# Nine layers in one kernel: the values products of attention in bursts of two key tiles, and four probability buffers in place of two

## The reference

```python
x = _layernorm(x + _L0_attn_ref(x, ...))     # recurrent mix
x = _layernorm(x + _L0_ffn_ref(x, ...))      # selected linear layer
x = _layernorm(x + _L1_attn_ref(x, ...))     # attention, no mask      (L = 0 in the kernel)
x = _layernorm(x + _L1_ffn_ref(x, ...))      # mixture of experts
x = _layernorm(x + _L2_attn_ref(x, ...))     # attention, causal       (L = 1)
x = _layernorm(x + _L2_ffn_ref(x, ...))      # attention, causal (L = 2), then a mixture
x = _layernorm(x + _L3_attn_ref(x, ...))     # attention, causal, with slopes (L = 3)
x = _layernorm(x + _L3_ffn_ref(x, ...))
# each attention, per block and head:
energy = jnp.einsum('bqhd,bkhd->bhqk', q, k) * scale
attn = jax.nn.softmax(energy, axis=-1)
out = jnp.einsum('bhqk,bkhd->bqhd', attn, v)
```

## Time and profile before

| | |
|---|---|
| median of three runs | 1397.71 us |
| span of the profiled execution | 1397.3 us |
| TensorE matmul busy | 1237.3 us (89%) |
| VectorE busy | 929.2 us (66%) |
| ScalarE busy | 712.3 us (51%) |
| mean granted TensorE clock | 0.957 of full speed |

### The profile page before, as it was taken

The page is one execution under the profiler, slowest core; times in us unless marked ns, Lnnn a source line. Parts: engine busy times, 40 slices in busy tenths (PEclk is TensorE's granted clock), DMA queues, the critical chain, the costliest instruction groups (busy, mean ns, idle before and its releaser), DMA issues.

```text
span 1397.3 us, 26983 instructions
## 1 busy us (share of the span) xinstructions
PE 1237.3 (89%) x8574; PEld 669.9 (48%) x8574; DVE 929.2 (66%) x2118; ACT 712.3 (51%) x1300; POOL 268.8 (19%) x557
## 2 busy tenths in 40 slices
PE   3445999999889998999999999999999979999876
PEld 1222223323356655455555555556665645555445
DVE  5867768686555556667767776755554576668676
ACT  2221777767544433656666666663222226666643
POOL 2342111111000012222322232110000211221112
PEclk7667999999999999999999999999999989999988
DMA  8212231310000003323323222100000202221000
GB/s 211 113 68 69 94 113 36 119 48 6 1 1 1 0 1 119 104 87 104 102 88 124 76 66 78 41 4 3 1 0 1 74 12 67 76 80 39 3 1 31
DMA packets 65199, 79.07 MB, mean 57 GB/s; under 512 B 5611, under 2 KB 58068, under 8 KB 64602
## 3 DMA queue, kind: packets, MB, share of 16 engines
q1 hardware_dynamic: 65098, 77.80, 17.6%
HBM read 45.17 MB, written 31.72 MB: 55 GB/s over the span
## 4 chain that ended last, share of the span: by engine, by line
PE 66%; issue 12%; DVE 8%; ACT 4%; DMA 3%; DVEq 3%; POOL 2%; POOLq 1%; SPq 1%; ACTq 0%
PE bank L1591 11%; PE bank L1605 11%; PE bank L1575 9%; PE bank L1757 6%; PE bank L1758 6%; PE bank L1775 5%; PE bank L1560 3%; PE bank L1578 3%; PE bank L1593 2%; DVE M L1175 2%; DMA KS<-scr_k 2%; PE bank L1625 2%; PE bank L1496 1%; PE bank L1490 1%; PE bank L1556 1%
## 5 line engine op out<-in xcount | busy, mean ns | idle before, releaser
L1175 DVE TENSOR_REDUCE M<-bank 128x1 f32<-128x512 f32 (+3 forms) x784 | 485.1, 653 | 191.7 <-PE bank L1578 133.4
L905 ACT ACTIVATE PT<-bank 128x512 f32<-128x512 f32 (+1 forms) x784 | 429.9, 569 | 258.5 <-PE bank L1593 186.7
L1575 PE MATMUL bank<-KS,QS 125*128 125x512 bf16 (+3 forms) x1024 | 308.0, 328 | 27.5 <-DVE M L1175 18.1
L1591 PE MATMUL bank<-QS,KS 128*128 128x512 bf16 (+3 forms) x1024 | 303.3, 323 | 13.6 <-ACT PT L905 7.5
L1605 PE MATMUL bank<-PT,VA 128*32 128x512 f32 (+3 forms) x2048 | 211.7, 485 | 1.6 <-ACT PT L905 1.0
L1591 PEld LDWEIGHTS bank<-QS,KS 128*128 128x128 bf16 x1024 | 99.3, 98 | 227.1 <-ACT PT L905 155.0
L1578 PE MATMUL bank<-maskb,identb 128*128 128x128 bf16 x768 | 151.4, 223 | 0.0
L1575 PEld LDWEIGHTS bank<-KS,QS 125*128 125x128 bf16 x1024 | 101.0, 99 | 101.5 <-DVE M L1175 46.0
L1593 PE MATMUL bank<-identb,maskb 128*128 128x128 bf16 x768 | 147.8, 219 | 0.0
L1775 PEld LDWEIGHTS bank<-MW,PT 128*128 128x128 f32 x864 | 111.8, 193 | 40.8 <-issue 38.2
L1757 PE MATMUL bank<-XT,MW 128*128 128x512 f32 (+1 forms) x232 | 120.6, 601 | 10.2 <-DVE PT L1349 5.9
(11 more groups left out here) (227 smaller groups left out, 1447.5 us busy)
## 6 DMA issues: line engine op xcount, KB each, us to landing
scr_q<-PQ SPq DMA_DIRECT2D x48, 384.0 KB, 3.2
QS<-scr_q SPq DMA_DIRECT2D x64, 288.0 KB
scr_k<-PK SPq DMA_DIRECT2D x24, 384.0 KB, 3.5
KS<-scr_k SPq DMA_DIRECT2D x32, 288.0 KB
QS<-MSB SPq DMA_DIRECT2D x192, 4.0 KB
MW<-in_m_w SPq DMA_DIRECT2D x3, 1024.0 KB, 9.5
MW<-in_m_w SPq DMA_DIRECT2D x3, 832.0 KB
scr_k<-PK SPq DMA_DIRECT2D x24, 96.0 KB, 1.9
```

The lines of the kernel that those rows point to most:

```text
L905: a.activation(PT[kt % 2][:, js[0]:js[-1] + 1, q0:T], tiles(bank[st_bank(L, g, i)][:, 0:w * len(js)], len(js)), ACT.Exp, scale=c["scale"]) ...
L1175: v.tensor_reduce(M[g % 2][:, t * GH + js[0]:t * GH + js[-1] + 1], tiles(bank[S_ORDER[L][i]][:, 0:kl * len(js)], len(js)), AX_X, ALU.max, ...
L1575: r = mm(s, QS[0:ROWS_SHIFT, g * GH + j, t * P:(t + 1) * P], KS[0:ROWS_SHIFT, kv_slot(L, g, j), 0:kl], start=True, stop=not causal)
L1591: r = mm(s, KS[:, kv_slot(L, g, j), kt * P:(kt + 1) * P], QS[:, g * GH + j, T - w:T], start=True, stop=not causal)
```

## The change

The probabilities get four buffers, one for each key tile, and the wait of ScalarE moves with them: key tile kt may be written once the product of tile kt of the unit before is done. The values products of tiles 0 and 1 are issued together at step 9, those of tiles 2 and 3 together at step 1 of the next unit. The two more buffers take 16 KB of each SBUF partition; the reserve for descriptors that GpSimd would write is cut to 1024 bytes to make room. All of the kernel's transfers are issued by SyncE.

```diff
+VALUES_HERE, VALUES_REST, VALUES_REST_AT = (0, 1), (2, 3), 1
-        PT = [sb(f"PT{i}", [P, GH, T]) for i in range(2)]
+        PT = [sb(f"PT{i}", [P, GH, T]) for i in range(NT)]
...
-                        at_least(act, pv_done, u * NT + kt - 1)
-                        a.activation(PT[kt % 2][:, js[0]:js[-1] + 1, q0:T],
+                        at_least(act, pv_done, u * NT + kt - 3)
+                        a.activation(PT[kt][:, js[0]:js[-1] + 1, q0:T],
...
-                        if prev and i == 1:
-                            values(*prev, NT - 1)
-                        for kt in range(NT - 1):
-                            if i == min(kt_end(L, kt) + 1, NI[L] - 1):
+                        if prev and i == VALUES_REST_AT:
+                            for kt in VALUES_REST:
+                                values(*prev, kt)
+                        if i == kt_end(L, VALUES_HERE[-1]) + 1:
+                            for kt in VALUES_HERE:
                                 values(L, b, g, kt)
...
                 if ends_chain(L):
-                    values(L, NB - 1, NG - 1, NT - 1)
+                    for kt in VALUES_REST:
+                        values(L, NB - 1, NG - 1, kt)
...
-    nc = bacc.Bacc("TRN2", target_bir_lowering=False, num_devices=1)
+    nc = bacc.Bacc("TRN2", target_bir_lowering=False, num_devices=1, dynamic_dma_scratch_size=1024)
```

More of the change, by code:

```diff
@@ L1604, in values @@
                 for j in range(GH):
-                    r = mm(bank[4][32 * j:32 * (j + 1), q0:T], VA[:, kt, kv_slot(L, g, j), :], PT[kt % 2][:, j, q0:T],
+                    r = mm(bank[4][32 * j:32 * (j + 1), q0:T], VA[:, kt, kv_slot(L, g, j), :], PT[kt][:, j, q0:T],
                            start=(kt == 0), stop=(kt == NT - 1))
```

## The result

The changed kernel takes 1421.5 us (median; 1414.3 to 1423.1) where the kernel before takes 1399.2 in the same rounds: a ratio of 1.0148, 95% interval [1.0117, 1.0179]. It is slower, by 21 us and not by the 10 of the forecast. The forecast's range ended at 1421, so the result lies at its upper edge: the median is just over it, and 1.0148 of the 1397.7 that the forecast started from is 1418.4. The profiled execution has a span of 1418.9 us, 21.6 more than the earlier trace rows.

A forecast was written before the change was run, and what follows sets the result against it. TensorE's stream was taken to set the time. Seams saved, less new waits and lost cover, made layer 0 +5.7 and causal layers +4.3: 1397.3 + 5.7 + 4.3 = 1407.3 us, range 1386 to 1421.

The forecast's parts named there:

- rival (c): Second product of a burst can't load weights beside the first's matmuls; each seam still costs about 0.1: 1420 us, chance 0.09.
- The seam: At each pair of values products, one entry (0.09) and exit (0.10) saved: 0.19 us, 126 times, 24 us.
- The forecast's own sign: If right, a pair's two products follow each other with 0.90 to 0.91 us between first starts, not 1.09.
- Layer 0's plain unit: Layer 0: new waits of 0.31 and 0.28 us outweigh two exits of 0.10: +0.39, about 13.55 us, not 13.17.
- the g = 0 units of blocks 0 to 2: Layer 0: tile 0's product no longer lies beside the wait for exp 7: +0.84 us, 3 units, 2.5 us.
- projections in layer 2: Causal units with rotary projections (g = 0, 7 units): TensorE is late throughout, -0.35 us each, 2.5 us gained.
- g = 2 with two norms: Causal, 6 units: tile 0's product now comes behind step 9, whose S waits for reduction 6: +0.8, 4.9 us.
- S at step 0 bound by a load: Layer 1, 5 units: tile 2's product now comes behind the KS load: +0.47 each, 2.4 us; layer 2, 0.3.
- (a): At every pair the seams win, with under half of 34 us of waits and lost cover: 1373 to 1390, chance 0.17.
- (b): Whole kernel: seams and waits cancel, the counted waits being 5 us too high: 1391 to 1404 us, chance 0.22.
- (d): The buffers matter because ScalarE could run ahead; held to gain nothing, given no time or chance of its own.
- two units with ST alone: Units with ST alone: layer 0's last two +0.6 us each (1.2), four causal ones +0.25 each (1.0).

The follow-up runs named there:

- e8: The changed kernel with SyncE issuing the key stacks' load ahead of the shift's for g of 2 and 3: 1402.9 us, ratio 1.0033 to before.
- e9: The kernel before with four buffers and the key stacks' load issued ahead of the shift's: 1393.4 us, ratio 0.9972 to before.
- e1: The kernel before with four buffers and the small descriptor reserve, every values product at its old step: 1399.8 us, ratio 0.9992 to before.
- e4: The changed kernel with the S of the same step between the two products of each pair: 1429.8 us, ratio 1.0198 to before.
- e10: Old order, four buffers, causal tiles 1 and 2 together at step 10, key stacks' load issued earlier: 1391.2 us, ratio 0.9940 to before.
- e12: e10 with tiles 1 and 2 together in layer 0 as well, at step 13: 1393.7 us, ratio 0.9951 to before.
- e3: Old order with four buffers, only tiles 2 and 3 together, at step 1 of the next unit: 1409.7 us, ratio 1.0056 to before.
- e2: Old order with four buffers, only tiles 0 and 1 together, at step 9: 1415.6 us, ratio 1.0101 to before.
- e7: Old order with four buffers, tiles 1 and 2 of the causal layers together at step 10: 1393.3 us, ratio 0.9966 to before.
- e13: e10 with causal tiles 1, 2 and 3 all at step 1 of the next unit: 1401.5 us, ratio 1.0012 to before.

## Why the prediction was right, and where it was not

The direction and the mechanism held: the seams close, and waits and lost cover cost more. The size is another matter. The forecast said +10 us and +21 came. The range reached that far only for rival (c), second products that pay their entry again, and (c) is refuted below. That the result lies at the range's edge is luck and no merit of the sum.

- **The seam** was put at 0.19 us, bounds 0 to 0.23; it is 0.24. The way out gives 0.15 and not 0.10: the issue of the eight matmuls is not paid by a second product in a burst. Rival (c), that each seam still costs 0.1, is refuted. So is, for these products, the rule weighed with it ("TensorE: Matmul & The Clock Gate", Part 3, the Trainium skill): all products use the same rows, and the second one's loads still cost nothing that the rows show. The forecast's own sign, 0.90 to 0.91 us between the two first starts, came out at 0.85. Its sentence that the trace agrees on the price of a change of tiling claims too much: the rule there names none, and the 0.24 us are the rows' alone.
- **Layer 0's plain unit** was put at 13.55 us and is 13.55. Two terms were off and cancelled: steps 2 to 9 wait 0.38 more (not 0.31), the two seams give 0.30 at the way out (not 0.20). The layer up to the start of its last unit came to +6.4 us (forecast +5.7 with that unit), and that is close by luck: the g = 0 units of blocks 0 to 2 gave 1.1 us (forecast 2.5), but the six units with g = 1 and g = 3 that were put at about 0 gave 3.1.
- **Causal layers, all but the load**: plain -0.10 in most, +0.06 in two (forecast -0.17), projections in layer 2 -0.28 to -0.42 (-0.35), g = 2 with two norms +0.75 (+0.8). Compared between e8 and e9, where the load is out of the way, the units of the two chains grow by +0.7 us in all; the forecast without its load terms was 4.3 - 2.7 = +1.6. In the 0.7, unit 62 alone stands for +1.6, which is the clock's (see the last point).
- **S at step 0 bound by a load** is the step that failed, by size: 5 units of +0.47 and 0.3, 2.7 us in all. From before to the changed kernel the units of the two chains grow by 12.7 us, from e9 to e8 by 0.7, so the load made 12.0 of it. The mechanism was named rightly (the load comes no sooner, tile 2's product comes behind it), but it was priced only where S already waited, and at the length of the product. Three things were left out. Units without a wait were taken as safe: in unit 39 the last packet had ended at 841.6 for a reader at 842.28, which is no slack at all where S starts 0.7 us behind the last packet. The landing was taken as fixed, where a 16 KB packet of the instruction queue can stand ahead of a load's last packets. The trace of before has one such case already (1226.02 to 1227.09, then six packets until 1227.73, 3.35 us after the issue was done), and it cost 0.33 us; in the changed kernel there is one in unit 39 and one from 1253.57 to 1255.09 ahead of the wait of 1.92 us in unit 56. And the clock: behind the waits of 2.94 us in u20 and 1.88 in unit 39 the granted clock is 0.50 for 3.4 us each.
- **The rivals**: (a), seams win, fell because waits and cover cost more than half of 34 us; (b), they cancel, is not what e8 shows: its +0.3% against before contains the early load's own gain. With the load early in both orders the new one costs 9.5 us, near the forecast's 10. (d), the buffers, is refuted by e1.
- **A smaller miss**: two units with ST alone, put at 0.6 and 0.25. Unit 15, with the mixture behind it, grew by 1.13 and unit 62 by 1.61; e8 keeps both (+1.03 and +1.35), so they are not the load's. Nor does the order of the products explain all of them: they go with a stretch at half clock. One of 3.4 us lies at the end of layer 0 (units 14 and 15, from 352.9 to 365.4) in the changed kernel, e1, e4, e8, e10 and e12 and one of 6.8 us in e3, but none in before, e2, e7, e9 and e13. In unit 62 half clock lasts 6.8 us in the changed kernel, e2, e7, e8 and e13, 3.4 us in before, e3, e4 and e9, and none is there in e1, e10 and e12.

How firmly the clock follows the wait: in u20 the wait for the load was 2.94, 2.86, 2.58 and 2.57 us in the changed kernel, e2, e3 and e4, and each has a stretch of 3.4 us at half clock there (from 621.5, 618.3, 619.5 and 624.8). With 1.29, 1.77 and 2.06 us in e7, before and e1 there is none, nor in e8, e9 or e10, where no such wait is. A wait for the shift's load can do it too: 1.85 us in unit 18 of e10 brought 3.4 us at half clock (from 592.2) and made that plain unit 1.26 us longer, while 1.75 us in e13 and 1.68 in e7 brought none. It isn't a rule by length alone: 1.88 us in unit 39 brought one, 2.07 and 1.92 in units 19 and 56 did not. What share of the 12 us is the clock's and what the wait's was not measured apart. An estimate from the rows: the load's waits fall by 16.5 - 4.8 = 11.7 us in the new order and by 8.3 - 4.7 = 3.6 in the old, which leaves 8.1, and two stretches of 3.4 us at half clock cost 1.7 each, 3.4 in all: 11.5 of the 12.0.

## What to carry to other kernels

A burst saves its seams, but what was under a wait comes out from under it; ask of each moved piece what it lay beside, and move only pieces that stand side by side already. A load that is just in time is a cost that the profile of before shows as zero: read the slack from the last packet to the first reader, not only the waits, count off the 0.7 us that passed here between the two, and take slack of less than a microsecond as spent. And look first at whether the load may be issued earlier, since that cures both orders, and here was the larger gain.

## Hardware behaviour that was not expected

- Entering and leaving the products' tiling (strips of 32 columns) costs 0.24 us: 0.09 on the way in, 0.15 on the way out; a second product of other operands in the same tiling costs 0.85 us for 512 columns.
- A load of the key stacks (two transfers issued by SyncE) lands 2.1 to 2.4 us after its issue is done in the like places of the changed kernel's execution (issue done at 755.5, 803.8 and 903.1), and took 3.8 at 852.4, where a 16 KB packet of the instruction queue, 1.06 us long, came ahead of its last six packets. The same pattern is in before at 1226 and in e7 at 1223.
- TensorE's next matmul starts 0.65 to 0.73 us behind the last packet of a load that it waits for (856.25 to 856.97; before, 1227.73 to 1228.46).
- A wait of 1.9 to 2.9 us on TensorE can cost 1.6 to 1.9 times its length, through 3.4 us at 1.2 GHz behind it, but does not always: 1.88 us brought it, 2.07 did not.
